# A Mamba mixer with a mixture of experts beside it: another way to pick the top two, another spread of scatters and gathers, a later start of the expert tiles

## What is computed

```python
xn = _layernorm(x)
# branch s: mamba, then mlp, each with a residual
xz = rmsnorm(xn) @ in_proj_w.T; xp, z = split(xz, 2)
xc = silu(causal_conv4(xp) + conv_b)
x_dbl = xc @ x_proj_w.T
dt = softplus(x_dbl[..., :16] @ dt_proj_w.T + dt_proj_b)      # B, C: the other 2 x 16 columns
h = h * exp(dt * A) + (dt * u) * B ; y = sum(h * C)           # a scan over 2048 tokens, 512 channels x 16 states
s1 = xn + ((y + xc * D) * silu(z)) @ out_proj_w.T
s = s1 + silu(rmsnorm(s1) @ mlp_w1.T) @ mlp_w2.T
# branch g: mixture of experts
gate_weights = softmax(xn @ gate_w + gate_b)                  # 8 experts
topk_values, topk_indices = jax.lax.top_k(gate_weights, 2)
hidden = relu(xn @ w1[e] + b1[e]); expert_out = hidden @ w2[e] + b2[e]
g = silu(sum(topk_values * expert_out[topk_indices]))
return x + s * g
```

## Time and profile before

| what | us |
|---|---|
| median of 3 runs (lowest, highest) | 1691.06 (1690.83, 1693.83) |
| the profiled execution, its own time | 1688.73 |
| its span in the profile | 1686.9 |
| TensorE busy | 1376.1 (82%) |
| VectorE busy | 1270.1 (75%) |
| GpSimd busy | 1191.7 (71%) |
| ScalarE busy | 909.1 (54%) |

### The profile page before, as it was taken

One profiled execution on the slowest core, in us unless ns is written; L12 is line 12 of the kernel. 1 busy time (PEld: TensorE's weight loads), 2 busy tenths in 40 slices (PEclk: granted clock), 3 DMA queues, 4 the chain that ended last, 5 costly groups with the idle time before them and its releaser, 6 DMA issues.

```text
span 1686.9 us, 17807 instructions
## 1 busy us (share of the span) xinstructions
PE 1376.1 (82%) x5328; PEld 1000.2 (59%) x5328; DVE 1270.1 (75%) x1545; ACT 909.1 (54%) x1967; POOL 1191.7 (71%) x619
## 2 busy tenths in 40 slices
PE   3565272988989898989899898899997989778677
PEld 1442022766677666766687666676776668645355
DVE  7469762887977897879778987889788968768522
ACT  3532333565575656665757565755756465535441
POOL 3523885775798679767797779767986798787830
PEclk9577775999999899989999999999999999879789
DMA  8713443754377436753486437544764447455530
GB/s 315 288 44 112 165 144 142 244 179 154 125 248 241 150 119 202 258 178 125 159 283 200 158 127 262 182 167 133 244 245 148 170 162 273 153 162 178 174 110 25
DMA packets 124321, 301.46 MB, mean 179 GB/s; under 512 B 14376, under 2 KB 26800, under 8 KB 113984
## 3 DMA queue, kind: packets, MB, share of 16 engines
q1 hardware_dynamic: 109200, 262.28, 45.8%
q0 software_dynamic: 9024, 27.27, 4.7%
q10 hardware_dynamic: 6000, 10.75, 1.9%
HBM read 258.57 MB, written 41.68 MB: 178 GB/s over the span
## 4 chain that ended last, share of the span: by engine, by line
PE 48%; DVE 13%; POOL 11%; ACT 9%; issue 9%; DMA 1%; DVEq 0%; SPq 0%; ACTq 0%; POOLq 0%
PE prod L909 38%; DVE state L1238 7%; PE ysum L961 5%; POOL dbu L644 4%; POOL slot_x L631 3%; POOL hxc L660 2%; ACT state L719 2%; DVE prod L1263 1%; DVE hxc L1249 1%; PE prod L914 1%; POOL late L691 1%; PE prod L1082 1%; ACT late L880 1%; PE prod L949 1%; DVE late L1309 1%
## 5 line engine op out<-in xcount | busy, mean ns | idle before, releaser
L1238 DVE TENSOR_TENSOR_SCAN state<-state,carry,dbu 128x512 f32<-128x512 f32 x512 | 657.8, 1285 | 218.6 <-ACT state L719 171.4
L644 POOL TENSOR_TENSOR dbu<-dtu,bb 128x1024 f32<-128x1024 f32 x256 | 602.5, 2360 | 81.5 <-DVE state L1238 76.4
L660 POOL TENSOR_TENSOR hxc<-hxc 128x1024 f32<-128x1024 f32 x164 | 386.6, 2357 | 246.9 <-DVE hxc L1249 246.8
L719 ACT ACTIVATE state<-dt,par 128x512 f32<-128x512 f32 x512 | 353.5, 692 | 106.2 <-DVE hxc L1249 91.0
L1249 DVE TENSOR_TENSOR hxc<-state,cb 128x512 f32<-128x512 f32 x512 | 354.3, 692 | 44.7 <-DVE state L1238 2.4
L909 PE MATMUL prod<-late 128*128 128x256 f32 x1248 | 302.6, 401 | 42.2 <-issue 15.6
L909 PEld LDWEIGHTS prod<-late 128*128 128x128 f32 x1248 | 256.5, 208 | 86.0 <-issue 46.3
L909 PE MATMUL prod<-xsT,late 128*128 128x256 f32 x1248 | 292.0, 386 | 9.7 <-DVE xc L1273 5.9
L909 PEld LDWEIGHTS prod<-xsT,late 128*128 128x128 f32 x1248 | 239.9, 194 | 65.9 <-issue 21.9
L961 PE MATMUL ysum<-hxc,ident 128*128 128x512 f32 x368 | 200.4, 673 | 84.0 <-POOL hxc L660 30.4
L717 ACT COPY carry<-state 128x1 f32<-128x1 f32 x384 | 61.3, 160 | 235.6 <-DVE hxc L1249 228.6
(11 more groups left out here) (152 smaller groups left out, 1263.2 us busy)
## 6 DMA issues: line engine op xcount, KB each, us to landing
bb<-bc_rows SPq DMA_DIRECT2D x256, 256.0 KB, 5.6
cb<-bc_rows SPq DMA_DIRECT2D x256, 256.0 KB, 4.1
late<-moe SPq DMA_DIRECT2D x39, 1028.0 KB, 4.9
late<-moe SPq DMA_DIRECT2D x39, 1024.0 KB, 5.3
slot_x<-xc POOLq DMA_DIRECT2D x20, 512.0 KB, 11.7
xs<-slot_x SPq DMA_DIRECT2D x39, 256.0 KB, 5.7
slot_y<-ys ACTq DMA_DIRECT2D x39, 256.0 KB, 3.5
late<-x SPq DMA_DIRECT2D x12, 512.0 KB, 8.6
```

Source lines behind the costliest of these rows:

```text
L644: nc.gpsimd.tensor_tensor(dbu[:, v % 3, :, :], dtu[:, n % 2, 2 * h:2 * h + 2, :], b, ALU.mult).then_inc(dbu_ready, 1)
L660: nc.gpsimd.tensor_tensor(hxc[:, to, :, :], hxc[:, to, :, :], hxc[:, piece, :, :], ALU.add).then_inc(summed, 1)
L719: nc.scalar.activation(state[:, k % 2, :], dt[:, n % 2, 2 * h + k % 2, :], ACT.Exp, scale=par[:, P_ALOG + col(k):P_ALOG + col(k) + 1]).the ...
L1238: nc.vector.tensor_tensor_scan(state[:, c, :], state[:, c, :], dbu[:, v % 3, c, :], carry[:, n % 2, col(k):col(k) + 1], ALU.mult, ALU.add) ...
```

## The change

Five things are changed.

- **The router's spread.** R_STEP goes from 1 to 2: TX and LG of a block every second step. R_AT goes from 10 to 18, so RO0 stands at step 18, BL at 22, RO7 at 26.
- **Top two.** RO2 and RO3 compared every pair of the eight probabilities (arrays of 128x2048) and added up ranks. Now each takes a maximum over the experts, a mask where it is reached, and, for ties, the first place in a table `place` (8, 7, ..., 1). RO3 first subtracts 2 where the first expert was taken. The load of `wm` on SyncE no longer waits for the router, as `wm` isn't scratch any more.
- **Scatters.** SC t stands at step 27 + 3t//2 (two SC in three steps), not at 19 + t: the last at step 73, not 50.
- **Tiles.** M_FROM goes from 52 to 80; M_TO stays 474. START stands at step 80.
- **Gathers.** For g = 0 to 4 the eight gathers stand in eight steps, G0 to G7 at GA + i. For g = 5 to 7 they stay together in the step GA. ScalarE's part of GA isn't moved.

```diff
-R_STEP, R_AT = 1, 10
+R_STEP, R_AT = 2, 18
-M_FROM, M_TO = 52, NK - 38
+M_FROM, M_TO = 80, NK - 38
@@ events()
-        out[R_AT + 9 + t].append(("R", "SC%d" % t, None))
+        out[R_AT + 9 + t * 3 // 2].append(("R", "SC%d" % t, None))
         out[at["GA"]].append(("D", "GA", g))
+        for i in range(2 * NT):
+            out[at["GA"] + (i if g < 5 else 0)].append(("D", "G%d" % i, g))
@@ sync
                 elif kind == "R" and name == "RO7":
-                    sp.wait_ge(routed, 2)
                     sp.dma_start(wm[:, :], mlp).then_inc(wm_in, 16)
@@ tensor, BL
-                    pe.wait_ge(router, 12)
+                    pe.wait_ge(router, 18)
@@ route()
-                elif piece == 2:
-                    nc.vector.tensor_tensor(c4, other, this, ALU.is_gt)
-                    step(nc.vector.tensor_tensor(t4, other, this, ALU.is_equal))
-                    step(nc.vector.tensor_tensor(t3, t3, eb, ALU.mult))
-                elif piece == 3:
-                    step(nc.vector.tensor_tensor(cmp, cmp, tie, ALU.add))
-                    step(nc.vector.tensor_reduce(rank, cmp.rearrange("p (t f) -> p t f", f=NE), AX_X, ALU.add))
-                    nc.vector.tensor_scalar(m0, rank, 0.0, None, ALU.is_equal)
-                    nc.vector.tensor_scalar(m1, rank, 1.0, None, ALU.is_equal)
-                    step(nc.vector.tensor_scalar(sel, rank, 1.5, None, ALU.is_lt))
-
-                    step(nc.vector.tensor_tensor(rank, m0, prob, ALU.mult))
-                    step(nc.vector.tensor_reduce(gates[:, 0, :], by_te(rank), AX_X, ALU.add))
-                    step(nc.vector.tensor_tensor(rank, m1, prob, ALU.mult))
-                    step(nc.vector.tensor_reduce(gates[:, 1, :], by_te(rank), AX_X, ALU.add))
+                elif piece in (2, 3):
+                    mask, left = ((m0, prob), (m1, rank))[piece - 2]
+                    best = gates[:, piece - 2, :]
+                    if piece == 3:
+                        step(nc.vector.scalar_tensor_tensor(out=rank, in0=m0, scalar=-2.0, in1=prob, op0=ALU.mult,
+                                                            op1=ALU.add))
+                    step(nc.vector.tensor_reduce(best, by_te(left), AX_X, ALU.max))
+                    step(nc.vector.tensor_tensor(by_te(mask), by_te(left), over_e(best), ALU.is_equal))
+                    step(nc.vector.tensor_tensor(mask, mask, place, ALU.mult))
+                    step(nc.vector.tensor_reduce(red, by_te(mask), AX_X, ALU.max))
+                    step(nc.vector.tensor_tensor(by_te(mask), by_te(place), over_e(red), ALU.is_equal))
+                    if piece == 3:
+                        step(nc.vector.tensor_tensor(sel, m0, m1, ALU.add))
```

More of the change, by code:

```diff
@@ L311, in mamba_moe @@
         eid = sb("eid", [P, ZTILES], I32)
-        cmp, tie = wm[:, 0:AT * NE * NE], wm[:, AT * NE * NE:2 * AT * NE * NE]
         xs_flat = xs[:, :, :, :].rearrange("p b r d -> p (b r d)")
@@ L322, in mamba_moe @@
         x1_flat = x1[:, :, :].rearrange("p t d -> p (t d)")
-        EARLY, GATEB, RED, CNT, COUNTS, NTILE, ENDS, BASE, STEPS, TI, EF = 0, 64, 72, 104, 112, 240, 248, 256, 264, 280, 328
-        earlier = x1_flat[:, EARLY:EARLY + NE * NE]
+        PLACE, GATEB, RED, CNT, COUNTS, NTILE, ENDS, BASE, STEPS, TI, EF = 704, 64, 72, 104, 112, 240, 248, 256, 264, 280, 328
+        place = x1_flat[:, PLACE:PLACE + AT * NE]
         gateb = x1_flat[:, GATEB:GATEB + NE]
@@ L457, in is_free @@
             return free_[USES[key][0]], 1
-        CONSTS = 15
+        CONSTS = 14
         NORM_STEPS = 7
@@ L599, in _, with iota @@
         def _(pool):
-            def iota(dst, pattern, cm=0):
-                nc.gpsimd.iota(dst, pattern, base=0, channel_multiplier=cm,
+            def iota(dst, pattern, cm=0, base=0):
+                nc.gpsimd.iota(dst, pattern, base=base, channel_multiplier=cm,
                                allow_small_or_imprecise_dtypes=True).then_inc(consts, 1)
@@ L604, in _ @@
             nc.gpsimd.memset(below[:, :], 0.0).then_inc(consts, 1)
-            nc.gpsimd.memset(earlier, 0.0).then_inc(consts, 1)
             nc.gpsimd.memset(seg, 1.0).then_inc(consts, 1)
-            pool.wait_ge(consts, 4)
+            pool.wait_ge(consts, 3)
             nc.gpsimd.affine_select(out=ident[:, :], in_=ident[:, :], compare_op=ALU.not_equal, fill=1.0,
@@ L612, in _ @@
                                     base=0, pattern=[[-1, P]], channel_multiplier=1).then_inc(consts, 1)
-            e3 = earlier.rearrange("p (e f) -> p e f", e=NE)
-            nc.gpsimd.affine_select(out=e3, in_=e3, compare_op=ALU.is_ge, fill=1.0,
-                                    base=0, pattern=[[-1, NE], [1, NE]], channel_multiplier=0).then_inc(consts, 1)
             nc.gpsimd.memset(seg.rearrange("p (e t) -> p e t", e=NE)[:, :, 0:1], 0.0).then_inc(consts, 1)
@@ L621, in _ @@
             iota(ti, [[1, ZTILES]])
+            iota(place, [[0, AT], [-1, NE]], base=NE)
             nc.gpsimd.memset(halo[:, :, :, :], 0.0).then_inc(consts, 1)
@@ L681, in do @@
                     scatter(int(name[2:]))
-                elif kind == "D" and name == "GA":
-                    g = i
-                    if g == 0:
+                elif kind == "D" and name[0] == "G" and name[1:].isdigit():
+                    g, t, k = i, int(name[1:]) // 2, int(name[1:]) % 2
+                    if g == 0 and t == 0 and k == 0:
                         for b in range(2):
                             pool.wait_ge(ys_out[b], 16 * ((TILES + 1 - b) // 2))
-                    if g >= 2:
+                    if g >= 2 and t == 0 and k == 0:
                         full(pool, (kind, "MX1", g - 2))
-                    for t in range(NT):
-                        for k in range(2):
-                            pool.indirect_dma_start(
-                                out=gy[g % 2][:, k, t, :], out_offset=None, in_=slot_y,
-                                in_offset=bass.IndirectOffsetOnAxis(ap=slots[:, k, g * NT + t:g * NT + t + 1], axis=0)
-                            ).then_inc(gathered[g % 2], 16)
+                    pool.indirect_dma_start(
+                        out=gy[g % 2][:, k, t, :], out_offset=None, in_=slot_y,
+                        in_offset=bass.IndirectOffsetOnAxis(ap=slots[:, k, g * NT + t:g * NT + t + 1], axis=0)
+                    ).then_inc(gathered[g % 2], 16)
             walk("pool", do)
@@ L1142, in over_t @@
                 return a.rearrange("p (a e) -> p a e", a=1).broadcast_to([P, n, NE])
-            c4 = cmp.rearrange("p (t e f) -> p t e f", e=NE, f=NE)
-            t4 = tie.rearrange("p (t e f) -> p t e f", e=NE, f=NE)
-            this = prob.rearrange("p (t e a) -> p t e a", e=NE, a=1).broadcast_to([P, AT, NE, NE])
-            other = prob.rearrange("p (t a e) -> p t a e", e=NE, a=1).broadcast_to([P, AT, NE, NE])
-            t3 = tie.rearrange("p (t f) -> p t f", f=NE * NE)
-            eb = earlier.rearrange("p (a f) -> p a f", a=1).broadcast_to([P, AT, NE * NE])
             counts = incl.rearrange("p (e t) -> p e t", e=NE)[:, :, AT - 1:AT].broadcast_to([P, NE, 16])
```

## The result

The changed kernel took 1710.51 us (median of four runs, 1708.59 to 1714.31) where the kernel before took 1690.94 beside it. The ratio is 1.0119, with a 95% interval of 1.0092 to 1.0146. The forecast was 1696.5, at most 1710. The sign was right, the size too small, and the time lies just outside the range.

The account below looks back on a forecast made before the run. GpSimd was taken to bound the scatters and gathers, TensorE the tiles between. The start and tiles gave -8 us and the last gather's order +13: +5, 1694 profiled, 1696.5 as median, range 1682 to 1710.

Parts of the forecast that it names:

- The logits: Router's logits, now every second step: 5 to 5.5 us a block, RO0 at 114.5 us (110 to 130) instead of 107.8.
- The router: RO0 to first scatter: cheaper top two shortens 48.2 us to 40.3, so the first scatter comes at 155 us.
- Rival 2: Logits stretch: TensorE never leaves the low clock, 8.6 us a block, RO0 14 to 18 us later; 1712 us; chance 0.13.
- the added 1 us for collisions: RO0 to first scatter: VectorE operations blocked by a GpSimd `dbu` on the shared port add 1 us, at most 9.
- The scatters: First to last scatter: GpSimd sets the pace, 151 us less about 2, last issued at 304 us.
- START: TensorE's START at 312 us, 30 later, 7.9 us after the last scatter, with SyncE in time.
- The gain of the later START: Tile stretch: 28.7 us of products moved ahead of START and 9 of gaps filled, M_TO at -8 us (-20 to +12).
- 9 of the 110 us of gaps: Tile stretch: denser tiles fill 9 us (0 to 20) of TensorE's 110 us of gaps.
- rival 1: Tile stretch: VectorE sets the pace in half of it, START at step 80 worth -18 us; 1681 us; chance 0.2.
- The gathers: Steps behind M_TO: spreading 40 gathers is the same GpSimd work and saves only holes; only G7 of g = 4 costs.
- The order at g = 4: Near the end: G7 of g = 4 behind all gathers of g = 5 delays MX by +13 us (+8 to +17), clock included.
- Rival 3: Near the end: G7 of g = 4 lands before TensorE needs it, so the order costs nothing; 1685 to 1691 us; chance 0.2.

Follow-up runs that it names:

- e4: The kernel before with M_FROM = 80 alone, router and scatters as before: 1676.96 us, ratio 0.9942.
- e1: The changed kernel with all eight gathers of every group together in step GA again: 1651.37 us, ratio 0.9785.
- e2: The kernel before with nothing but the spread of the gathers of g = 0 to 4: 1746.49 us, ratio 1.0354.
- f2: The changed kernel with the gathers of g = 0 to 4 two per step, not one: 1654.11 us, ratio 0.9799.
- f3: The changed kernel, gathers still one per step, with MX, GT, FI and ST of g = 0 to 4 four steps later: 1661.88 us, ratio 0.9857.
- e3: The changed kernel with the gathers of g = 4 together, those of g = 0 to 3 still spread: 1685.82 us, ratio 0.9999.
- g3: The changed kernel with gathers in bursts except those of g = 4, which stay one per step: 1671.06 us, ratio 0.9900.
- h1: The changed kernel with MX, GT, FI and ST of g = 0 to 4 four steps later and the gathers of g = 4 together: 1650.45 us, ratio 0.9777.
- h2: The changed kernel with gathers in bursts and tiles from step 86 instead of 80: 1652.05 us, ratio 0.9776.

## Why the prediction was wrong, point by point

- **The logits: price right, moment wrong. The router: right.** I had a block at 5 to 5.5 us and RO0 at 114.5, at the earliest 110. From the first LG (64.82) to the last (101.19) it was 5.2 us a block: TensorE had no wait from 64.8 us on and ran at the high clock from 72.6 (LG in 1.85 us). But RO0 came at 107.96, as early as before. The 114.5 doesn't follow from the price: the first LG stands at 65.00 in the kernel before too, and eight blocks of 5.25 from there end at 107. Rival 2 was wrong. From RO0 to the first scatter it took 40.8 us, predicted 40.3. The collisions with `dbu` are there: VectorE's softmax product at 112.26 took 1.30 us, its update at 120.44 took 2.13 and a product at 140.65 took 1.40, against 0.42 for their likes, and each ended 0.3 us behind a `dbu`:

```profile
112.26 1.30 DVE L1155 TENSOR_TENSOR xs<-xs,x 128x256 f32<-128x256 f32 x1
...
120.44 2.13 DVE L1160 SCALAR_TENSOR_TENSOR xs<-ys,xs 128x256 f32<-128x256 f32 x1
...
140.65 1.40 DVE L1190 TENSOR_TENSOR ys<-ys,xsT 128x256 f32<-128x256 f32 x1
```

```profile
110.93 2.35 POOL L641 TENSOR_TENSOR dbu<-dtu,bb 128x1024 f32<-128x1024 f32 x1 [5.38 <-DVE state L1225]
119.94 2.34 POOL L641 TENSOR_TENSOR dbu<-dtu,bb 128x1024 f32<-128x1024 f32 x1 [6.66 <-DVE state L1225]
...
139.42 2.35 POOL L641 TENSOR_TENSOR dbu<-dtu,bb 128x1024 f32<-128x1024 f32 x1 [8.26 <-DVE state L1225]
```

  Together they cost 3.6 us, as much as in the kernel before (its two in the earlier trace rows, and a product at 146.20 of 1.40 us), so the added 1 us for collisions measured 0. The exclusive lock of the Trainium skill (page "SBUF — State Buffer", section "SBUF: two separate sides") fits all three: the operation that came second waited for the first to end. By that rule the bound was 9 us; the trace has these three and stays far from it. A fourth may be the scan at 129.75 (1.96 us for 128x256, where a step's scan of 128x512 takes 1.28): a `dbu` stood over it in every run, so none shows what it takes alone.
- **The scatters: right.** 150.3 us from the start of the first (148.76) to the end of the last (299.02), predicted 149. GpSimd was busy for 133 of the 150 us in the window above.
- **START: right, by luck: two errors cancel.** The last scatter ended 5 us earlier than said (299.0, not 304), since RO0 came early, but START came 12.1 us behind it, not 7.9: SyncE issued the first load of `xs` only at 303.65, behind loads of `bb` and `cb` at 301.43 and 301.80. I had called SyncE in time. The idle time named as a sign (15 to 30 us ahead of START) was 5.16 us; TensorE's long idle time, 32.18 us, lay further ahead, from 260 to 292, at an ACC whose ADD stood among the scatters on GpSimd. START's row:

```profile
311.08 1.12 PE L909 MATMUL prod<-ident,xs 128*128 128x128 f32 x4 [5.16 <-DMA xs<-slot_x]
```

- **The gain of the later START: mechanism right, size too small.** The term "9 of the 110 us of gaps" measured 20.8, and a second, of 15.6 us for TensorE at the low clock, was missing. That is more than rival 1, which took half of the stretch as VectorE's; M_TO came 36 us earlier and not 18, and the gaps, rival 1's sign ("well below 90 us"), measured 86.6. e4 shows that it is the change of M_FROM alone: START +54.8, the stretch -65.0.
- **The gathers: the step that failed.** "The 40 spread ones are the same work; GpSimd is the bound of this stretch, so the spread saves only the holes in which it waited." I counted GpSimd's work and asked who stood behind whom for one gather, G7 of g = 4. I didn't ask it for the groups ahead, though one link of the ring stands in the prediction ("VectorE's last step is held behind the finish of g = 3"). So the spread of g = 0 to 3 was priced at nothing, and it cost 35 us. There the last gather moved from nine steps ahead of MX to two, behind ADDs that wait for VectorE, and VectorE waits for the MX of the group before at FI. e1, e2, f2 and f3 show the ring and its 35 us; e3 and g3 show that it isn't in g = 4.
- **The order at g = 4: mechanism right, size too small.** MX of g = 4 was 11.4 us late in g3, predicted 13. "Up to there the clock gets a longer pause as well, within that range" was the mis-sized part: 7.3 us more until OUT, and some 20 in all.
- **The signs that I had named pointed the wrong way.** MX of g = 3 at 1567.16 (predicted 1566), G7 issued at 1600.92 (1603), MX of g = 4 at 1603.70 (1606) behind a wait of 13.24 us: all near the forecast, since the 28 us that the tile stretch gained more were by then lost to the ring. A moment that comes out as forecast doesn't prove the terms in front of it. The time from one fixed step to the next does.
- **Rival 3** (the order costs nothing) was wrong, as g3 shows.

What stays open: how much of the ring's 35 us is the waits and how much the clock. TensorE's busy time accounts for 25 (114.5 against 89.6 us), but the longer products also lengthen the waits of silu and FI (each second half of an MX held silu for 5.72 us), and no run held the clock while keeping the waits. Nor is it shown why the tile stretch fills 21 us of gaps; the density of the tiles and the place of the freed products were never tried apart.

## What to carry to other kernels

Spreading a burst of DMA issues through an in-order queue also spreads them behind everything that this queue waits for: count the steps between the **last** of them and its reader, and follow the reader's result around all queues back to the issuing one. Here two steps closed a ring that cost 35 us and six left it open at no cost, with the same instructions. An early barrier such as START belongs at the step where its data lands, with as much other work as there is in front of it in the queue; and when a wait is moved onto TensorE, price the products behind it at the low clock too, which here added two thirds to the wait. The changed kernel with its gathers in bursts again takes 0.9785 of the time before; no other run was faster beyond the noise (h1 0.9777, h2 0.9776).
